# 256-channel deformable slots: early corners behind the last weighted sums, late corners in the first three taps, the first block's side rows over two taps

## The chip, the cores and the metric

One core of one Trainium2 chip. The metric is the device time of the whole kernel in microseconds. The core has five engines that run side by side and meet at semaphores: TensorE (PE), VectorE (DVE), ScalarE (ACT), GpSimd (POOL) and the DMA queue of SP.

## What is computed

Four layers follow each other on an input of 2 x 256 x 64 x 64 in float32: attention with a group norm, a positional term, a deformable bottleneck of 64 channels, and, as layer 3, two deformable convolutions of 256 channels. The change touches only layer 3, which is, for each of the two images:

```
h = relu(group_norm(x, gn1))
h = deform_conv(h, dw1, pw1, pwb1, w1, b1)
h = relu(group_norm(h, gn2))
h = deform_conv(h, dw2, pw2, pwb2, w2, b2)
return h + x
```

A deform_conv first makes two offsets for each of 9 taps at each pixel (a 7x7 depthwise convolution times a 1x1 one). Tap k is then read at a shifted, fractional place: the four pixels around it, each weighted by its share. The output is the product of the 9 x 256 sampled values with w (256 x 256 x 9).

## The kernel before

**Turns.** Layer 3 runs as four turns of `products256` (TensorE), `copies256` (ScalarE), `sums256` (VectorE) and `gathers256` (GpSimd): turn 0 is image 1 with the first deform_conv, turn 1 image 0 with the first, turn 2 image 1 with the second, turn 3 image 0 with the second. Between two turns all engines meet: each drains and signals, and SP lets them go (`meet`, L377 for SP). After the barrier VectorE works out the group norm of the image just made (`group_norm`, L1643), with one product by TensorE (L767) and one root by GpSimd (`inverse_root`, L582) inside; turn 3 needs none. SP starts the loads of a turn after its barrier: 4 MB of residual before turns 2 and 3, 2.3 MB of weights before turns 0 and 2.

**A tap.** A turn has 8 blocks of 512 pixels, a block 9 taps (k = 0 to 8), 72 taps in all. For a tap GpSimd issues four indirect gathers (`gathered`, L690, issue L696), each of which fetches for 128 pixels the four corners of 256 channels (0.5 MB). There are twelve gather tiles `G3`, three taps' worth, so the gathers of tap j + 3 are issued when tap j has been used (`half_done`) and ScalarE has copied their indices into `IS3` (L1475, semaphore `is_ready`). ScalarE multiplies the first corner by its weight (L1466), VectorE adds the other three (L2052: twelve instructions a tap, two halves of six), TensorE turns the result round (`transposes`, L1145), ScalarE copies that out of PSUM (`staged`, L1484), and TensorE multiplies it by the weights (`tap`, L1155, eight instructions a tap). The body of a tap on TensorE (`staged_tap`, L1163) is: wait for the copies of tap j, transposes of tap j + 1, a piece of the side work, matmuls of tap j. ScalarE is written tap by tap in order: products of tap j, copies of tap j - 1, side work. After a block's last tap ScalarE evicts the output (`output`, L1494 or L1499) and VectorE takes statistics of it (L2065) or adds the residual (L2040).

**Side work.** Turns 0 to 2 also prepare the next turn (`side`), one block at a time: ScalarE normalises the next image (L1355, L1369) and copies tiles of it (L1359, L1367), TensorE transposes those for the gather table (`side_table3`, L1032, two parts) and makes the offsets' 14 rows (`side_rows3`, L1040, two instructions each), VectorE adds the rows up shifted (`side_shifts3`, L1928 and L1934, waits for row 14), TensorE moves them to pixels (L984), VectorE adds them to the base (L1944). Block 0 of the side work is done before tap 0 of TensorE (`products256`: two table parts, all 14 rows, then the transposes of tap 0), block n + 1 beside block n.

**Corners.** VectorE turns offsets into whole indices and weights: `corner_floors` (L1731 to L1748, six instructions), `corner_indices` (L1754, L1758), `corner_weights` (L1766 to L1785, five). Each instruction waits for the one before. They come in two parts, `EARLY = 5`: blocks 0 to 4 of the next turn, and blocks 5 to 7. The early part is done in the last block of a turn, after taps 3, 4 and 6 (`early_corners`, L2074; in turn 0 also the two offset weights, L1886, after taps 2 and 3). The late part is done in the second block of the next turn, after taps 0, 2 and 5 (`late_corners`, L2087). Turn 0's own corners are done ahead of it. With the early indices there (`corners_done`), ScalarE copies in its last three taps the indices of the next turn's taps 0 to 2, and GpSimd issues their twelve gathers, from the next table (`following`), before it goes to the barrier.

Of the kernel before, what the change touches and what calls it, by code (L numbers as in the profile page):

```python
# [21 lines left out]
CH = C // 128  # L22
# [7 lines left out]
KK = 9  # L30
# [16 lines left out]
def program(nc, x, wqkv, wproj, pos_l, pos_r, vec, vec64, w1, woff, boff, w2, w3, dw, pw, wd,  # L47
            ident, mean32, mean8, sel2, sel3, base2, base3, out):
    ctx = ExitStack()
    with ctx:  # L50
# [512 lines left out]
        def _(pool):  # L563
# [136 lines left out]
            def gathers256(b, begins, following):  # L700
# [56 lines left out]
        def _(pe):  # L757
# [379 lines left out]
            def products256(side, new_weights=False):  # L1137
# [35 lines left out]
                def beside(n, k, first, ahead, last):  # L1173
# [4 lines left out]
                    if k == 2:  # L1178
# [5 lines left out]
                    if k >= 2 and not last:  # L1184
# [37 lines left out]
            products256(0, True)  # L1222
# [3 lines left out]
            products256(1)  # L1226
# [3 lines left out]
            products256(0, True)  # L1230

            meet()
            products256(None)
# [5 lines left out]
        def _(act):  # L1239
# [121 lines left out]
            def side_opening(b):  # L1361

                for n in range(2):
                    for half in range(CH):
                        at = chunk(n)
                        if n == 0:
                            af(NS3[:, half, :], INNER[b][:, half, at], ACT.Relu,  # L1367
                               scale=gsc[:, half:half + 1], bias=gbi[:, half:half + 1]).then_inc(ns_ready, 1)
                        af(INNER[b][:, half, at], INNER[b][:, half, at], ACT.Relu,  # L1369
                           scale=gsc[:, half:half + 1], bias=gbi[:, half:half + 1]).then_inc(stage_ready, 1)  # L1370
                for part in range(2):
                    side_copy3(part)
                for half in range(CH):
                    side_tile(b, 1, half)
# [76 lines left out]
            def copies256(b, turn, layer, side):  # L1451
# [5 lines left out]
                def products(i, k, wraps=False):  # L1457
# [44 lines left out]
                def beside(n, k, first, ahead, last):  # L1502
# [6 lines left out]
                    if 5 <= k <= 6 and ahead:  # L1509
                        side_tile(side, n + 2, k - 5)  # L1510

                def nine(g, first=False, second=False, ahead=True, last=False):

                    for k in range(KK):
                        if k > 0 or not first:
                            products(3 * g + k // 3, k % 3, last and side is not None and k >= KK - 3)
# [6 lines left out]

                weights(0, 0)
                if turn == 0:
                    af(IS3.rearrange("p a t -> p (a t)"), IDX3[:, 0:12], ACT.Copy).then_inc(is_ready, 3)
                    side_opening(side)
                products(0, 0)
                if turn == 1 or turn == 2:
                    act.wait_ge(gn_ready, 1)  # L1530
                    act.sem_inc(gn_ready, -1)
                    side_opening(side)
# [6 lines left out]
                staged(2)  # L1539
                output(NCH - 1)  # L1540
# [33 lines left out]
        def _(dve):  # L1574
# [459 lines left out]
            def sums256(b, layer, side, side_layer=0):  # L2034
# [39 lines left out]
                def early_corners(k):  # L2074

                    if k == 2 or k == 3:
                        if b == 1 and layer == 0:
                            offset_weights(1, k - 2)
                    if k == 3:
                        floors3(0, EARLY)  # L2080
                    if k == 4:
                        indices3(0, EARLY)
                        dve.sem_inc(corners_done, 1)
                    if k == 6:
# [165 lines left out]
```

## Time and profile before

| | us |
|---|---|
| median of three runs | 5462.92 |
| lowest and highest of them | 5460.71, 5473.15 |
| the profiled execution: its time | 5466.21 |
| its span | 5464.4 |

| engine | busy us | share of the span |
|---|---|---|
| TensorE matmuls | 5005.7 | 92% |
| VectorE | 4056.5 | 74% |
| GpSimd | 3392.1 | 62% |
| ScalarE | 2415.0 | 44% |

The profile is one execution; the times of its rows are in us from the span's start. The four turns fill the last third of the span, from about 3616 to 5464: turn 0 goes to about 4094, turn 1 to 4575, turn 2 to 5056. A timeline row gives start, length, engine, line, operation, operands, count, and in brackets how long the engine had been idle before it and what released it; instructions of one kind are merged in a row, so that neighbours may overlap by some 0.1 us. A windows row gives a stretch, its length, the busy time of TensorE matmuls, TensorE weight loads, VectorE, ScalarE and GpSimd (with the number of instructions), the granted TensorE clock (1.00 is 2.4 GHz, 0.50 is 1.2), the busy share of the DMA engines and what they moved in GB/s.

### The profile page before, as it was taken

Reading aid. Unit: us, or ns where it says so; the run is one execution under the profiler, and the core shown is the slowest. Engines: PE = TensorE matmul, PEld = TensorE weight load, DVE = VectorE, ACT = ScalarE, POOL = GpSimd, SP = SyncE. Lnnn points to the kernel's source line nnn. Section 1 sums busy time; section 2 is a strip of 40 time slices with the busy share of each in tenths; the row PEclk is TensorE's granted clock in tenths of the full one; section 3 lists DMA queues with packets and bytes.
Section 4 is the critical chain, followed back from the end, with each engine's and each line's share of the span. In section 5 each row is a group of like instructions: output and inputs, shape, how many; then the busy total and the mean of one; then the engine's idle time right before and its main releaser. Section 6 shows DMA issues by size and latency. Waiting matters only on the chain. (4 is left out here: it accounts for less than half of the span.)

```text
span 5464.4 us, 75029 instructions
## 1 busy us (share of the span) xinstructions
PE 5005.7 (92%) x23052; PEld 2329.0 (43%) x23052; DVE 4056.5 (74%) x6532; ACT 2415.0 (44%) x4301; POOL 3392.1 (62%) x2919
## 2 busy tenths in 40 slices
PE   7999999999799999999978869969998997999888
PEld 3333333333333333333336656745544554554444
DVE  4888888885488888888533334458987897998898
ACT  2455555554245554555411111125544554554555
POOL 0676777766067677777627757746654564666675
PEclk9999999999899999999968879989999999999999
DMA  2000000000100000000044435569997998999998
GB/s 74 1 1 1 1 1 1 1 1 16 48 1 1 1 1 1 1 1 1 2 107 120 128 106 157 164 221 385 370 361 297 375 375 331 382 383 378 385 410 356
DMA packets 320000, 812.09 MB, mean 149 GB/s; under 512 B 69934, under 2 KB 137396, under 8 KB 319470
## 3 DMA queue, kind: packets, MB, share of 16 engines
q0 software_dynamic: 193536, 679.59, 33.2%
q1 hardware_dynamic: 126190, 129.07, 7.0%
q8 instruction: 145, 2.38, 0.2%
q14 instruction: 129, 1.06, 0.1%
HBM read 708.09 MB, written 100.43 MB: 148 GB/s over the span
## 5 line engine op out<-in xcount | busy, mean ns | idle before, releaser
L647 POOL TENSOR_TENSOR arena<-arena 128x512 f32<-128x512 f32 x960 | 1438.4, 1498 | 576.6 <-ACT arena L1281 495.8
L696 POOL DMA_INDIRECT arena<-corners,arena x1152 | 1101.0, 956 | 695.4 <-DVE arena L2052 332.7
L1813 DVE TENSOR_REDUCE arena<-ps 128x2 f32<-128x1024 f32 x1024 | 1252.2, 1223 | 354.7 <-PE ps L806 351.7
L1281 ACT ACTIVATE arena<-ps 128x1024 f32<-128x1024 f32 x1024 | 1045.9, 1024 | 1061.0 <-PE ps L832 1033.5
L2052 DVE SCALAR_TENSOR_TENSOR ps<-arena,ps 128x256 f32<-128x256 f32 x2304 | 956.5, 484 | 178.8 <-DVEq L2046 170.8
L1155 PE MATMUL ps<-arena 128*128 128x512 f32 x2304 | 1060.8, 604 | 0.2
L832 PE MATMUL ps<-arena 64*128 64x512 f32 x4096 | 1046.0, 589 | 0.0
L845 PE MATMUL ps<-arena 128*64 128x512 f32 x4096 | 991.3, 605 | 0.0
L1835 DVE TENSOR_TENSOR arena<-arena 128x512 f32<-128x512 f32 x960 | 877.9, 914 | 104.4 <-ACT arena L1281 102.9
L684 POOL DMA_INDIRECT arena<-corners,arena x576 | 547.0, 950 | 276.9 <-issue 246.2
L1466 ACT ACTIVATE ps<-arena 128x256 f32<-128x256 f32 x1152 | 499.0, 469 | 473.1 <-DVE arena L2052 190.5
L1155 PEld LDWEIGHTS ps<-arena 128*128 128x128 f32 x2304 | 437.3, 195 | 502.3 <-issue 501.4
L2052 DVE SCALAR_TENSOR_TENSOR arena<-arena,ps 128x256 f32<-128x256 f32 x1152 | 499.6, 476 | 0.0
L845 PEld LDWEIGHTS ps<-arena 128*64 128x64 f32 x4096 | 248.5, 136 | 583.0 <-issue 354.3
L832 PEld LDWEIGHTS ps<-arena 64*128 64x128 f32 x4096 | 390.4, 187 | 241.5 <-issue 159.9
L1145 PE MATMUL ps<-ident_s,arena 128*128 128x128 f32 x2304 | 332.5, 280 | 151.0 <-DVE arena L2052 141.6
L1970 DVE TENSOR_TENSOR arena<-arena,ps 128x2304 f32<-128x2304 f32 x64 | 163.5, 2554 | 401.3 <-DMA arena<-corners,arena 401.0
L1484 ACT ACTIVATE arena<-ps 128x512 f32<-128x512 f32 x576 | 308.7, 586 | 234.9 <-ACTq L1482 231.4
L1145 PEld LDWEIGHTS ps<-ident_s,arena 128*128 128x128 f32 x2304 | 265.5, 143 | 344.8 <-DVE arena L2052 211.5
L828 PE MATMUL ps<-arena 64*128 64x512 f16 x2048 | 389.1, 377 | 18.7 <-ACT arena L1281 18.7
L806 PE MATMUL ps<-arena 64*128 64x512 f16 x2048 | 394.4, 382 | 4.8 <-DVE arena L1813 2.7
L806 PEld LDWEIGHTS ps<-arena 64*128 64x128 f16 x2048 | 98.5, 93 | 587.0 <-DVE arena L1813 529.2
(169 smaller groups left out, 3865.0 us busy)
## 6 DMA issues: line engine op xcount, KB each, us to landing
corners<-arena SPq DMA_DIRECT2D x256, 256.0 KB
arena<-corners,arena POOLq DMA_INDIRECT x1728, 7.7
img<-in_x SPq DMA_DIRECT2D x8, 1024.0 KB, 9.3
corners<-arena SPq DMA_DIRECT2D x128, 64.0 KB, 2.2
arena<-in_wd SPq DMA_DIRECT2D x2, 2304.0 KB, 8.5
between<-img SPq DMA_DIRECT2D x4, 1024.0 KB, 6.3
arena<-between SPq DMA_DIRECT2D x4, 1024.0 KB, 9.1
resid<-img SPq DMA_DIRECT2D x8, 512.0 KB
```

The lines of the kernel that those rows point to most:

```text
L647: pool.tensor_tensor(SUMS[u % 2][:, 0, :], SUMS[u % 2][:, 0, :], P[n % 4][:, 0, :], ALU.add).then_inc(sum_a, 1)
L684: pool.indirect_dma_start(G2[q][:, k, :], None, table64[b], bass.IndirectOffsetOnAxis(ap=IS2[:, q, k:k + 1], axis=0)).then_inc(g2_ready[q] ...
L696: pool.indirect_dma_start(G3[4 * k + t].rearrange("p a c -> p (a c)"), None, table256[b], bass.IndirectOffsetOnAxis(ap=IS3[:, k, t:t + 1], ...
L832: last = mm(ps[:, 2 * (n % 2) + h, :], KF[u // QB][rows, kc * 128:(kc + 1) * 128], QF[u // QB][rows, (u % QB) * CHUNK:(u % QB + 1) * CHUNK ...
L845: last = mm(ps[64 * h:64 * h + 64, 6, :], V[:, kc, at:at + 64], P[n % 4][:, h, :], start=(kc == 0), stop=(kc == NT - 1), tile_position=(0, ...
L1145: last = tr(ps[:, 2 + half, t * 128:(t + 1) * 128], SAMP[k][:, t, half * 128:(half + 1) * 128], ident_s[:, :])
L1155: last = mm(ps[:, 6 + oh, :], WD[:, k, half, oh * 128:(oh + 1) * 128], ST[k % 3][:, half, :], start=(k == 0 and half == 0), stop=(k == KK ...
L1281: af(P[n % 4].rearrange("p h q -> p (h q)"), ps[:, 2 * (n % 2):2 * (n % 2) + 2, :].rearrange("p h q -> p (h q)"), ACT.Exp, scale=float(D) ...
L1466: af(ps[:, h, (t % 2) * C:(t % 2 + 1) * C], G3[4 * k + t][:, 0, :], ACT.Copy, scale=WS3[:, k, 4 * t:4 * t + 1]).then_inc(prod_ready, 1)
L1813: v.tensor_reduce(mxp[u % 2][:, :, t, j], ps[:, 4:6, :], AX.X, ALU.max).then_inc(mx_done, 1)
L1835: v.tensor_tensor(SUMS[u % 2][:, 1, :], SUMS[u % 2][:, 1, :], P[n % 4][:, 1, :], ALU.add).then_inc(sum_b, 1)
L2052: last = v.scalar_tensor_tensor(SAMP[k][:, t, :] if corner == 3 else acc, G3[4 * k + t][:, corner, :], WS3[:, k, 4 * t + corner:4 * t + co ...
```

## The change

The early corners (and in turn 0 the offset weights) go behind the last weighted sum of the turn, and ScalarE copies the twelve indices at once when they are there, so that the next turn's first twelve gathers are issued after that. The late corners go into the first block, after taps 0, 1 and 2. In the first block of turns 1 and 2 TensorE begins with the transposes of tap 0; block 0's fourteen side rows go into taps 0 and 1, seven each, the wait for the shifts from tap 2 to tap 4, and block 1's rows into taps 4 to 8, three each; VectorE's shifts go from tap 1 to tap 3 and the offsets from tap 7 to tap 8; ScalarE normalises block 1 after the table copies, and copies its tile after tap 2's products. Turn 3, which has no side work, also takes its tap 0 transposes first, as before. The core of the diff:

```diff
@@ gathers256 (GpSimd) @@
-                if following is None:
-                    pool.wait_ge(is_ready, 3)
-                    pool.sem_inc(is_ready, -3)
-                else:
+                if following is not None:
                     for k in range(3):
@@ products256, beside (TensorE) @@
+                    spread = first and turn > 0
+                    if spread and k < 2:
+                        side_rows3(side, 0, range(7 * k, 7 * (k + 1)))
-                    if k == 2:
+                    if k == (4 if spread else 2):
                         side_shifts_done()
                         if ahead:
                             side_normal_done(CH)
                     if k == (5 if first else 4):
                         side_shifted(T3[0], 7, O3, sel3_s)
-                    if k >= 2 and not last:
+                    if k >= 4 and spread:
+                        side_rows3(side, n + 1, range(3 * (k - 4), min(14, 3 * (k - 3))))
+                    if k >= 2 and not spread and not last:
                         side_rows3(side, n + 1, range(2 * (k - 2), 2 * (k - 1)))
@@ products256, opening (TensorE) @@
+                if turn > 0:
+                    transposes(0, 0)
                 if side is not None:
                     side_table3(0)
                     side_table3(1)
                     side_normal_done(2 * CH)
+                if turn == 0:
                     side_rows3(side, 0, range(14))
-                transposes(0, 0)
+                    transposes(0, 0)
@@ side_opening (ScalarE); with_tile is False in turns 1 and 2 @@
+                for half in range(CH):
+                    af(NS3[:, half, :], INNER[b][:, half, chunk(0)], ACT.Relu,
+                       scale=gsc[:, half:half + 1], bias=gbi[:, half:half + 1]).then_inc(ns_ready, 1)
+                for half in range(CH):
+                    side_normal(b, 0, half)
+                if not with_tile:
+                    for part in range(2):
+                        side_copy3(part)
+                for half in range(CH):
+                    side_normal(b, 1, half)
+                if with_tile:
+                    for part in range(2):
+                        side_copy3(part)
                     for half in range(CH):
-                        at = chunk(n)
-                        if n == 0:
...
+                        side_tile(b, 1, half)
@@ copies256 (ScalarE) @@
-                    ahead = 3 * i + k + 3
-                    if wraps:
-                        ahead = 3 * i + k + 3 - TAPS
-                        if ahead == 0:
-                            act.wait_ge(corners_done, 1)
-                            act.sem_inc(corners_done, -1)
-                    af(IS3[:, k, :], IDX3[:, bass.ds(ahead * 4, 4)], ACT.Copy).then_inc(is_ready, 1)
+                    if not ends:
+                        af(IS3[:, k, :], IDX3[:, bass.ds((3 * i + k + 3) * 4, 4)], ACT.Copy).then_inc(is_ready, 1)
...
+                    if first and turn > 0 and k == 2:
+                        for half in range(CH):
+                            side_tile(side, 1, half)
...
                 staged(2)
+                if side is not None:
+                    act.wait_ge(corners_done, 1)
+                    act.sem_inc(corners_done, -1)
+                    first_indices()
                 output(NCH - 1)
@@ sums256 (VectorE) @@
+                def early_corners():
+
+                    floors3(0, EARLY)
+                    indices3(0, EARLY)
+                    dve.sem_inc(corners_done, 1)
+                    weights3(0, EARLY)
+                    if b == 1 and layer == 0:
+                        for half in range(CH):
+                            offset_weights(1, half)
 
                 def late_corners(k):
 
                     if k == 0:
                         floors3(EARLY, NCH)
+                    if k == 1:
+                        indices3(EARLY, NCH)
                     if k == 2:
-                        indices3(EARLY, NCH)
-                    if k == 5:
                         weights3(EARLY, NCH)
 
+                begins = not (b == 1 and layer == 0)
...
-                        if second and not (b == 1 and layer == 0):
+                        if first and begins:
                             late_corners(k)
                         if side is not None:
-                            if k == 1:
+                            if k == (3 if first and begins else 1):
                                 side_shifts3(side_layer)
-                            if last:
-                                early_corners(k)
-                            if k == 7:
+                            if k == (8 if first and begins else 7):
                                 side_offsets3(g)
...
-                nine(NCH - 1, last=True)
+                if side is not None:
+                    early_corners()
```

`first_indices` is the one copy of `IDX3[:, 0:12]` into `IS3` that turn 0 has at its start already (L1526); it signals `is_ready` by 3.

## Rows read from the trace of the kernel before

**Rows 1.** Windows, one block each: length, engine busy us, granted clock, DMA share, GB/s.
```profile
4251.10:4307.80 56.70, 54.68 (x189) 28.95 (x188) 49.38 (x119) 31.21 (x81) 32.79 (x35) 0.97 0.97 374
4516.40:4575.00 58.60, 49.53 (x164) 25.08 (x163) 54.91 (x131) 27.21 (x72) 33.55 (x36) 0.94 0.93 341
5126.50:5175.60 49.10, 41.68 (x143) 21.30 (x142) 47.85 (x124) 28.21 (x76) 34.03 (x35) 0.97 1.02 401
5223.50:5270.80 47.30, 41.75 (x146) 20.31 (x144) 44.64 (x111) 27.74 (x76) 34.69 (x36) 1.00 1.03 409
```

**Rows 2.** Timeline, VectorE, last blocks of turns 0 and 1: start, us, instruction.
```profile
4053.80 1.07 DVE L1886 TENSOR_TENSOR arena<-dw_s,pw_s 128x882 f32<-128x882 f32 x1
...
4541.99 0.34 DVE L1731 TENSOR_SCALAR arena<-arena 128x360 f32<-128x360 f32 x1
...
4545.65 1.66 DVE L2052 SCALAR_TENSOR_TENSOR ps<-arena,ps 128x256 f32<-128x256 f32 x4 [0.26 <-DVEq L2046]
...
4551.55 0.33 DVE L1754 SCALAR_TENSOR_TENSOR arena<-arena 128x180 f32<-128x180 f32 x1
...
4552.86 1.66 DVE L2052 SCALAR_TENSOR_TENSOR ps<-arena,ps 128x256 f32<-128x256 f32 x4 [0.36 <-DVEq L2046]
...
4562.27 0.34 DVE L1766 TENSOR_SCALAR arena<-arena 128x360 f32<-128x360 f32 x1
...
4565.34 1.66 DVE L2052 SCALAR_TENSOR_TENSOR ps<-arena,ps 128x256 f32<-128x256 f32 x4 [0.26 <-DVEq L2046]
```

**Rows 3.** Timeline, VectorE, between turn 0 and turn 1.
```profile
4093.27 0.87 DVE L2052 SCALAR_TENSOR_TENSOR arena<-arena,ps 128x256 f32<-128x256 f32 x2
...
4106.95 0.60 DVE L1646 BATCH_NORM_AGGREGATE mv<-bnst 128x2 f32<-128x48 f32 x2 [1.87 <-DVEq L1874]
...
4112.59 1.66 DVE L2052 SCALAR_TENSOR_TENSOR ps<-arena,ps 128x256 f32<-128x256 f32 x4 [0.35 <-DVEq L2046]
```

**Rows 4.** Timeline, GpSimd, between turn 0 and turn 1.
```profile
4110.60 0.71 POOL L582 TENSOR_TENSOR grs<-grs,minus_half 128x2 f32<-128x2 f32 x1 [13.12 <-POOLq L581]
```

**Rows 5.** Timeline, start of turn 0: VectorE, ScalarE, GpSimd.
```profile
3615.88 0.35 DVE L1731 TENSOR_SCALAR arena<-arena 128x360 f32<-128x360 f32 x1
...
3619.90 0.47 DVE L1758 CAST arena<-arena 128x180 int32<-128x180 f32 x1
...
3629.92 0.20 ACT L1526 ACTIVATE arena<-arena 128x12 int32<-128x12 int32 x1
...
3631.14 1.00 POOL L696 DMA_INDIRECT arena<-corners,arena  x1 [16.34 <-POOLq L705]
...
3645.00 0.95 POOL L696 DMA_INDIRECT arena<-corners,arena  x1 [0.30 <-DVE arena L2052]
```

**Rows 6.** Timeline, GpSimd, last block of turn 0, beside corner weights.
```profile
4081.55 1.06 POOL L696 DMA_INDIRECT arena<-corners,arena  x1 [0.30 <-issue]
```

**Rows 7.** Timeline, TensorE, first block of turn 1.
```profile
4115.04 1.08 PE L1032 MATMUL ps<-ident_s,arena 128*128 128x128 f32 x4 [6.02 <-PEq L1028]
...
4118.48 13.18 PE L1040 MATMUL ps<-img,arena 128*126 128x512 f32 x28
...
4142.90 6.03 PE L1155 MATMUL ps<-arena 128*128 128x512 f32 x8
...
4190.94 1.88 PE L1040 MATMUL ps<-img,arena 128*126 128x512 f32 x4
...
4192.65 3.60 PE L1155 MATMUL ps<-arena 128*128 128x512 f32 x8
...
4196.09 1.04 PE L1145 MATMUL ps<-ident_s,arena 128*128 128x128 f32 x8
```

**Rows 8.** Timeline, ScalarE and VectorE, first block of turn 1.
```profile
4114.65 2.21 ACT L1369 ACTIVATE img<-img,gbi,gsc 128x512 f32<-128x512 f32 x3
...
4121.44 1.65 ACT L1466 ACTIVATE ps<-arena 128x256 f32<-128x256 f32 x4
...
4132.66 4.58 DVE L1934 SCALAR_TENSOR_TENSOR arena<-ps,sel_s,arena 126x488 f32<-126x488 f32 x6
```

More of the change, by code:

```diff
@@ L1135, in products64, with products256 @@
                 four(NCH - 1, ahead=False, last=True)
-            def products256(side, new_weights=False):
+            def products256(side, turn, new_weights=False):
                 def transposes(tap, k):
@@ L1221, in _ @@
             meet()
-            products256(0, True)
+            products256(0, 0, True)
             meet()
             gn_means(mean8_s)
-            products256(1)
+            products256(1, 1)
             meet()
             gn_means(mean8_s)
-            products256(0, True)
+            products256(0, 2, True)
             meet()
-            products256(None)
+            products256(None, 3)
             meet()
@@ L1359, in side_tile, with side_opening @@
                 af(NS3[:, half, :], INNER[b][:, half, chunk(n)], ACT.Copy).then_inc(ns_ready, 1)
-            def side_opening(b):
-                for n in range(2):
-                    for half in range(CH):
-                        at = chunk(n)
-                        if n == 0:
[L1367 to L1374, printed above, removed]
+            def side_opening(b, with_tile=True):
+                for half in range(CH):
[11 more added lines that the diff above has]
+                        side_copy3(part)
+                    for half in range(CH):
+                        side_tile(b, 1, half)
             def side_copy(to, width, begins, ends):
@@ L1455, in weights, with products @@
                     af(WS3[:, k, :], W4_3[:, bass.ds(j * 16, 16)], ACT.Copy).then_inc(act_step, 1)
-                def products(i, k, wraps=False):
+                def products(i, k, ends=False):
                     act.wait_ge(act_step, 1)
@@ L1515, in nine @@
                         if k > 0 or not first:
-                            products(3 * g + k // 3, k % 3, last and side is not None and k >= KK - 3)
+                            products(3 * g + k // 3, k % 3, last and k >= KK - 3)
                         if k > 0 or not first:
@@ L1522, in nine, with first_indices @@
                             beside(g, k, first, ahead, last)
+                def first_indices():
+                    af(IS3.rearrange("p a t -> p (a t)"), IDX3[:, 0:12], ACT.Copy).then_inc(is_ready, 3)
                 weights(0, 0)
                 if turn == 0:
-                    af(IS3.rearrange("p a t -> p (a t)"), IDX3[:, 0:12], ACT.Copy).then_inc(is_ready, 3)
+                    first_indices()
                     side_opening(side)
@@ L1531, in copies256 @@
                     act.sem_inc(gn_ready, -1)
-                    side_opening(side)
+                    side_opening(side, False)
                 nine(0, first=True)
@@ L1539, in copies256 @@
                 staged(2)
+                if side is not None:
+                    act.wait_ge(corners_done, 1)
+                    act.sem_inc(corners_done, -1)
+                    first_indices()
                 output(NCH - 1)
@@ L2072, in residual_back @@
                     dve.sem_inc(x_back, -64)
[L2074 to L2084, printed above, removed]
-                        weights3(0, EARLY)
+                def early_corners():
[6 more added lines that the diff above has]
+                            offset_weights(1, half)
                 def late_corners(k):
@@ L2090, in late_corners, with nine @@
                         floors3(EARLY, NCH)
+                    if k == 1:
+                        indices3(EARLY, NCH)
                     if k == 2:
-                        indices3(EARLY, NCH)
-                    if k == 5:
                         weights3(EARLY, NCH)
-                def nine(g, first=False, second=False, last=False):
+                begins = not (b == 1 and layer == 0)
+                def nine(g, first=False):
                     for k in range(KK):
@@ L2117, in sums256 @@
                     residual_back()
-                nine(1, second=True)
-                with dve.Fori(2, NCH - 1) as g:
+                with dve.Fori(1, NCH) as g:
                     nine(g)
-                nine(NCH - 1, last=True)
+                if side is not None:
+                    early_corners()
                 if layer == 1:
```

## The prediction, made before the changed kernel was run

> **What bounds it now.** I read the windows view first, over one block (nine taps) of each kind. In a middle block of turn 1 TensorE is busy 54.7 of 56.7 us and the DMA engines at 0.97; in turn 3, which prepares nothing for a next turn, VectorE is busy 44.6 of 47.3 us and the DMA engines at 1.03 [rows 1]. So a middle block gives nothing to an edit of VectorE. The edges of the turns are different, and I read them in the timelines, engine by engine. In the last block of turn 1 TensorE falls to 49.5 of 58.6 us while VectorE is busy for 54.9: there VectorE sets the pace, and the corner instructions stand between its weighted sums [rows 2]. Behind the last sum comes the stretch in which only the end of the product runs, then the barrier and the group norm [rows 3]. GpSimd has by then issued the next turn's twelve gathers and sits idle, 13.1 us before its root [rows 4]. After the barrier comes a first block in which TensorE opens late [rows 7]. I count from T, the end of turn 0's last weighted sum (4094.1), and M, VectorE's first instruction behind the barrier (4106.95): M = T + 12.8 now, and the first weighted sum of turn 1 starts at M + 5.6 [rows 3].
>
> **Corners out of the last block.** In turn 1 VectorE leaves its sums for 3.66 us (floors), 1.31 (indices; the statistics in front stay) and 3.07 (weights), together 8.0 us [rows 2]. In turn 0 the two offset-weight products of 1.07 us go too, with their semaphore steps some 1.3 each: 10.7. VectorE is the pace-setter, has no wait between these rows, and TensorE has 9 us to spare in the block [rows 1], so I take the whole: -10.7 -8.0 -8.0 = **-26.7 us**. It can't be more. It can be less if the gathers don't keep up: at turn 3's 47.3/9 = 5.25 us a tap instead of VectorE's 4.70 (two halves of 2.35, a row of 1.66 and one of 0.87 less their overlap [rows 3]), seven taps lose 3.9 us a block, which gives 15 us as the lower end.
>
> **Corners behind the last sum.** The 7.4 us of VectorE itself (10 with the offset weights) are free: it now idles there until the last eviction at T + 9.7. What they release is not. The order becomes: floors and indices, ScalarE's copy of twelve indices, twelve gathers on GpSimd, and only then GpSimd's arrival at the barrier, because gathers256 issues all twelve before it returns. All of this stands in the trace once, at turn 0's start [rows 5]: floors and indices 3615.88 to 3620.37, 4.5 us; copy 0.2 us, and first gather 1.0 us after it; first to last gather 13.9, and the last takes 0.95. With 0.35 from VectorE to ScalarE the last gather ends at T + 4.5 + 0.35 + 0.2 + 1.0 + 14.8 = T + 20.8. From the last arrival to M the trace has 1.9 us [rows 3], so M moves from T + 12.8 to T + 22.7: +9.9 us, at three transitions **+29.7 us**. Queued behind those gathers is the root of the group norm, on the same engine [rows 4], and behind it VectorE, ScalarE and TensorE, so nothing covers the wait. At the third transition SP's residual fetch moves with the barrier too. The ends are 9.1 us (a wake-up of 0.2 in place of 1.0) and 11 (as much again for the drain), so 27 to 33. ScalarE's new wait is over at T + 4.9, and behind it only the last evictions are queued, which TensorE releases after T + 7.
>
> Here a rule speaks against the change. In the trace a gather beside the corner weights takes 1.06 us in place of 0.95 [rows 6], so I add nothing for the weights that now run beside the twelve gathers. The Trainium skill, SBUF — State Buffer, section "Who interferes with whom", has VectorE and GpSimd share a port pair under an exclusive lock, the loser blocking for the whole instruction. By the trace the sum gets under 1 us from this; by the rule more, which is a rival below.
>
> **First block of turns 1 and 2.** TensorE sets its length. From M to the end of tap 8's matmuls it takes 4196.09 - 4106.95 = 89.1 us. Its work, at full clock: nine taps of 3.44; ten sets of transposes of about 0.88; 28 side rows, two in 1.71; four table parts of 0.44; 0.8 for the shifted offsets [rows 7]: 66.2. So 22.9 us are lost, 9.5 of them before the fourteen rows start at M + 11.5 and the rest in waits and a slow stretch (the matmuls of tap 1 took 6.0 us in place of 3.6). The change puts the transposes of tap 0 first, and they need its sums, which end at M + 10.4, so TensorE reaches the tables at M + 11.0, where it now does at M + 8.1 [rows 7]. From there the two tables with the copy between them take 3.4 us, as now (4115.04 to 4118.48). ScalarE, which works in order, needs 3.0 us from the end of the second table to the products of tap 1 (4121.44 [rows 8]) with a copy, two tile copies and one normalisation between; it will have a copy and three normalisations (0.74 each [rows 8]), some 3.3. So the products start at M + 17.7, VectorE has the first half 1.1 later, and tap 1 goes from about M + 18.8 to M + 23.5, 3.3 us later after M than now. The rows, in the body of tap 0 behind the transposes of tap 1, start at M + 24.0, with 2.6 us of the work done: 21.4 us lost. Add 1.1 for their slow opening (28 instructions took 13.2 us, at 0.43 each 12.0). From there TensorE is continuous to tap 2's matmuls: rows to M + 31.1, tap 0 to 34.5, transposes 35.4, rows to 41.4, tap 1, transposes, a table part and tap 2 to 49.7. VectorE's shifts wait for row 14 and take 5.4 us (0.8 and 4.6 [rows 8]), to M + 47; ScalarE's products of tap 4 follow its first table copy, so tap 4's sums last from about M + 48.3 to 53.0, and TensorE stands some 3.5 us. The second table copy holds tap 5's products in the same way: 3.5 more, 7 in all. Lost in all 29.5 against 22.9: +7 us a turn, **+14 us**. With none of the later waits it is 0, with a slow clock for one more tap +10: 0 to +20 over both turns.
>
> The late corners (about 6.9 us of VectorE) leave the second block, where TensorE hides them: nothing. In the first block of turns 1 and 2 they lie beside TensorE's rows: nothing.
>
> **Turn 3 and the rest.** There the late corners cost now: the second block takes 49.1 us against 47.3 [rows 1]. In the first block they delay when slots come free, while the DMA engines bring 4 MB of residual first (10 us at 409 GB/s) and hide most of it. Between -1.8 and +5, I take 0. Turn 0's first block keeps its order; only the table tile of block 0 comes 0.7 us earlier on ScalarE: 0.
>
> **Sum:** -26.7 + 29.7 + 14 + 0 = +17.0 us. The profiled execution has a span of 5464.4 and a time of 5466.2 us, 3.3 above the median of the three runs shown; I put the change on the median: 5462.9 + 17.0 = **5479.9 us**. From here on, faster and slower mean by over 0.2% (10.9 us), about what a measurement of this kernel tells from no change.
>
> **Rivals.**
> (a) The first blocks cost nothing: spreading the rows lets TensorE recover all it loses at the opening. For it: VectorE's taps 2 and 3 no longer wait for the shifts. Against: TensorE is the bound, and opens its rows 12 us later. -26.7 + 29.7 = +3.0: 5465.9.
> (b) Faster: the barrier does not move. Its place is GpSimd's arrival; if the twelve gathers cost it no time, M stays at T + 12.8 and -26.7 + 14 = -12.7 gives 5450.2. It decides from an added wait of 0.6 us a transition or less (-26.7 + 14 + 1.8 = -10.9). Against it stand 14.8 us for twelve gathers, and the root behind them.
> (c) The last blocks stay bound by data, as turn 3 is: they give 15 in place of 26.7, +11.7: 5491.6.
> (d) VectorE's corner weights (3.1 us [rows 2]) and in turn 0 the offset weights (2.1) keep GpSimd from issuing while they run: 3 x 3.1 + 2.1 = 11.4 us of later barriers, 5491.3. Against it is the row of 1.06 us [rows 6]. That is what the rule of the Trainium skill named above (SBUF — State Buffer) would do here.
>
> **Chances.** Forecast 0.60, (a) 0.20, (b) 0.05, (c) 0.08, (d) 0.07. About 0.05 of the forecast's own 0.60 lies under 5473.8, where both first blocks come out near their lower end. So slower 0.55 + 0.08 + 0.07 = 0.70, same 0.25, faster 0.05. The range reaches from just under (a) to just over (c) and (d), which also takes in the forecast with its first blocks at +20 and its barriers at 33 (-26.7 + 33 + 20 = 26.3, 5489): 5464 to 5495.
>
> **What would show it.** Right: no corner instruction among the last block's sums, and that block at about 50.6 us; twelve gathers between T + 6 and T + 21; the root's idle time small before the gathers and the first group-norm instruction near T + 22.7; in turns 1 and 2 TensorE's rows starting at M + 24 and tap 8 ending near M + 96. Wrong: a first group-norm instruction before T + 17, or a first block under 89 us.

## The result, and the profile after

The changed kernel takes **5501.82 us** (median of four runs, 5499.76 to 5503.2) where the kernel before took 5463.19 beside it: 1.0067 times as long (95% interval 1.005 to 1.0084), 38.6 us slower. The forecast was 5479.9 in a range of 5464 to 5495. The direction was right; the loss is 2.3 times the forecast one.

The profiled execution of the changed kernel has a span of 5501.1 us, 36.7 above the one before. No engine does more work:

```profile
span 5501.1 us, 75087 instructions
PE 5003.4 (91%) x23052; PEld 2332.9 (42%) x23052; DVE 4055.7 (74%) x6532; ACT 2412.9 (44%) x4292; POOL 3385.3 (62%) x2919
```

So all of it is waiting. The windows view, block by block as in [rows 1]: a middle block of turn 1, its last block, and the second and fourth blocks of turn 3.

```profile
4267.80:4324.50 56.70, 54.68 (x189) 28.62 (x188) 49.37 (x119) 31.17 (x81) 32.71 (x36) 0.97 0.99 384
4532.30:4581.90 49.60, 46.02 (x167) 24.09 (x165) 49.04 (x119) 26.75 (x69) 23.79 (x26) 1.00 0.85 330
5165.30:5213.50 48.20, 42.40 (x147) 20.66 (x145) 44.74 (x112) 27.65 (x75) 35.28 (x38) 1.00 1.03 410
5260.80:5308.10 47.30, 41.70 (x146) 20.30 (x144) 44.60 (x111) 27.68 (x76) 34.74 (x36) 1.00 1.03 410
```

The last block is 49.6 us in place of 58.6, with VectorE busy for 49.04 of them: it still sets the pace, without the corner work. What was gained there is lost at the barrier. The timeline of VectorE between turn 0 and turn 1, against [rows 2, 3]:

```profile
4085.63 0.86 DVE L2066 SCALAR_TENSOR_TENSOR arena<-arena,ps 128x256 f32<-128x256 f32 x2
4086.41 0.34 DVE L1745 TENSOR_SCALAR arena<-arena 128x360 f32<-128x360 f32 x1
...
4090.42 0.48 DVE L1772 CAST arena<-arena 128x180 int32<-128x180 f32 x1
...
4096.53 1.29 DVE L2079 BATCH_NORM_STATS2 bnst<-img 128x6 f32<-128x512 f32 x2
4117.26 0.60 DVE L1660 BATCH_NORM_AGGREGATE mv<-bnst 128x2 f32<-128x48 f32 x2 [19.43 <-DVEq L1888]
...
4122.90 1.66 DVE L2066 SCALAR_TENSOR_TENSOR ps<-arena,ps 128x256 f32<-128x256 f32 x4 [0.35 <-DVEq L2060]
```

The last sum ends at T = 4086.49, the floors and indices behind it take until 4090.9, the last statistics are done at 4097.8, and then VectorE stands for 19.4 us: M = 4117.26 = T + 30.8, where the forecast had T + 22.7. (At the barrier before turn 3, which has no group norm, M is ScalarE's first instruction behind it.) GpSimd in the same stretch, against [rows 4, 5]:

```profile
4092.33 1.09 POOL L696 DMA_INDIRECT arena<-corners,arena  x1 [16.91 <-POOLq L711]
...
4106.26 0.95 POOL L696 DMA_INDIRECT arena<-corners,arena  x1 [0.30 <-issue]
4120.91 0.71 POOL L582 TENSOR_TENSOR grs<-grs,minus_half 128x2 f32<-128x2 f32 x1 [13.70 <-POOLq L581]
```

The twelve gathers stand where they were forecast, T + 5.8 to T + 20.7. But M doesn't follow the last of them by 1.9 us, it follows by 10.0. In between only their data moves, as 2-us windows show (the last two columns are the DMA engines' share and GB/s); its last packet ends at 4112.6:

```profile
4110.00:4112.00 2.00, 0.00 (x0) 0.00 (x0) 0.00 (x0) 0.00 (x0) 0.00 (x0) 0.50 0.93 373
4112.00:4114.00 2.00, 0.00 (x0) 0.00 (x0) 0.00 (x0) 0.00 (x0) 0.00 (x0) 0.50 0.02 6
```

The kernel before has nearly the same distance. Its twelfth gather ends at 4097.49, and its M of 4106.95 [rows 3] is 9.5 us behind that:

```profile
4096.54 0.95 POOL L696 DMA_INDIRECT arena<-corners,arena  x1 [0.30 <-issue]
```

TensorE and ScalarE at the opening of turn 1, against [rows 7, 8]:

```profile
4128.65 1.06 PE L1029 MATMUL ps<-ident_s,arena 128*128 128x128 f32 x4
...
4141.75 7.57 PE L1037 MATMUL ps<-img,arena 128*126 128x512 f32 x14
...
4210.73 3.60 PE L1152 MATMUL ps<-arena 128*128 128x512 f32 x8
```
```profile
4134.99 1.65 ACT L1474 ACTIVATE ps<-arena 128x256 f32<-128x256 f32 x4
```

Counted from M: the first table 11.4 (forecast 11.0), tap 1's products 17.7 (17.7), the rows 24.5 (24.0), the end of tap 8's matmuls 97.1 (96).

**Where the 36.7 us come from**, by T, M and the end of each block's evictions on ScalarE in both traces:

| term | forecast | measured |
|---|---|---|
| last blocks of turns 0, 1, 2, to T | -26.7 | -10.7 -8.1 -8.0 = -26.8 |
| barriers, M - T | +29.7 | 12.8, 12.9, 12.9 to 30.8, 29.9, 30.6: +52.7 |
| first blocks of turns 1 and 2, from M | +14 | +7.7 +7.8 = +15.5 |
| all else | 0 | -4.7 |

The last line is -7.9 in the second to seventh blocks (-3.1 in the second blocks of turns 1 and 2; -3.4 in their sixth, which ran 56.6 us at a granted clock of 0.97 before and 54.9 at 1.00 after; the rest in turn 3), +0.6 in turn 0's first block and turn 3's edges, and +2.6 at the start of the layer and behind the last eviction, outside all edits. The barrier's term is 23 us off, and that is the miss.

### The profile page after: what moved, and what is told of

Same layout as the page of the kernel before. It is cut to its first block and busy times, and to the rows that moved or that the text cites. A ratio compares the mean times of both kernels' runs of the same rounds, so it can differ in the third digit from the quotient of the medians.

```text
span 5501.1 us, 75087 instructions
## 1 busy us (share of the span) xinstructions
PE 5003.4 (91%) x23052; PEld 2332.9 (42%) x23052; DVE 4055.7 (74%) x6532; ACT 2412.9 (44%) x4292; POOL 3385.3 (62%) x2919
## 5 line engine op out<-in xcount | busy, mean ns | idle before, releaser
L1152 PE MATMUL ps<-arena 128*128 128x512 f32 x2304 | 1047.5, 598 | 0.2
```

The lines of the kernel that those rows point to most:

```text
L1152: last = mm(ps[:, 6 + oh, :], WD[:, k, half, oh * 128:(oh + 1) * 128], ST[k % 3][:, half, :], start=(k == 0 and half == 0), stop=(k == KK ...
```

## The experiments

The theory after this reading: `drain` in GpSimd's `meet` doesn't end before the data of the gathers ahead of it has landed. Rivals: the drain takes a fixed time behind the last issue, or another engine arrives late. Medians are given with their ratio to the kernel before, run on the same chip; M and T are read from each run's trace.

**No drain.** At the three barriers behind the gathers GpSimd arrives with a plain increment:

```diff
-                pool.drain().then_inc(arrived, 1)
+                pool.sem_inc(arrived, 1)
```

> The changed kernel, with GpSimd signalling its arrival at the three barriers between the turns without draining first. T is the end of a turn's last weighted sum, M the first group-norm instruction behind the barrier; in the changed kernel M = T + 30.8, 29.9 and 30.6, while the last of the twelve gathers has been issued at T + 20.7 and the gathers' data ends at about T + 25.5. Theory 'landing' (GpSimd's drain holds until the data of its gathers is there) and theory 'fixed' (the drain takes some 8 us behind an indirect DMA, whatever the data): M = T + 22.6 at each, 8 us less three times, so 24 us under the changed kernel, about 5478. Theory 'other engine' (something else arrives last): M stays at T + 30, 5502.

5474.96 us, 1.0021 (1.0011 to 1.0031), 27 below the changed kernel. M - T is 12.2 and 12.5 at the first two barriers and 17.1 at the third. At the first two the barrier's whole loss is GpSimd's drain, and no other engine is late. At the third 4 us are left, and they are SP's: before it arrives, it waits until the last output store has landed (`fo_sent`, L541). SP issued that store here:

```profile
5066.16 1.12 SPq L490 DMA_DIRECT2D out_y<-img  x2
```

Its packets share the DMA engines with the gathers' and end at 5074.0, with M at 5074.8; in the kernel before they end at 5068.3, with M at 5069.2. The drain's removal isn't all gained, because the root of the group norm now stands behind the gathers. VectorE and GpSimd, turn 0 to 1:

```profile
4099.59 0.60 DVE L1663 BATCH_NORM_AGGREGATE mv<-bnst 128x2 f32<-128x48 f32 x2 [0.86 <-DVEq L1891]
...
4109.04 0.16 DVE L1691 TENSOR_TENSOR gsc<-grs,vec_s 128x2 f32<-128x2 f32 x1 [5.89 <-DVEq L1690]
```
```profile
4107.20 0.94 POOL L699 DMA_INDIRECT arena<-corners,arena  x1 [0.30 <-issue]
4108.16 0.73 POOL L582 TENSOR_TENSOR grs<-grs,minus_half 128x2 f32<-128x2 f32 x1
```

The first weighted sum is at M + 10.6 in place of M + 5.6. The wait has moved from the barrier to the root.

**A quarter of the bytes.** Drain kept; each of the twelve gathers ahead of the barrier fetches a quarter of its row, so the first three taps of turns 1 to 3 are computed from other data:

```diff
-                        G3[4 * k + t].rearrange("p a c -> p (a c)"), None, table256[b],
+                        G3[4 * k + t].rearrange("p a c -> p (a c)")[:, 0:part * C], None,
+                        table256[b].rearrange("r (q c) -> (r q) c", c=part * C),
```

> The changed kernel, its drain kept, with each of the twelve gathers ahead of a barrier fetching a quarter of the bytes (one corner's worth of each row, so the first three taps of turns 1 to 3 are computed from other data). The number of gathers and their issue times stay. Theory 'landing': the data ends some 2 us behind the last issue, M = T + 20.7 + 2 + 5.2 = T + 28, about 3 us less three times, 9 us under the changed kernel: 5493. Theory 'fixed': M stays at T + 30.5, 5502. A later start of tap 1 or 2 isn't expected under either.

5498.43 us, 1.0061 (1.0044 to 1.0078). The total falls between the two theories. By the trace M - T is 28.8, 27.9 and 27.6, so 2.0, 2.0 and 3.1 us less, while the data ends 3.5 to 4.4 us earlier, counted from T. It moves with the landing, but not by the full amount: open until the crowded runs below.

**The first block as before.** Only TensorE's, ScalarE's and VectorE's order in the first blocks is undone:

```diff
-                    spread = first and turn > 0
+                    spread = False
...
-                            if k == (3 if first and begins else 1):
+                            if k == 1:
```

> The changed kernel with the first block of turns 1 and 2 as before the change (side rows ahead of the transposes of tap 0, shifts after tap 1, ScalarE's opening in one piece); early corners behind the last sum and late corners in taps 0 to 2 stay. From M to the first eviction the changed kernel takes 95.5 and 95.9 us, the kernel before 87.8 and 88.1. If the order of the opening is what costs: 15.5 us under the changed kernel, 5486. If it is the late corners beside the first taps, or the colder TensorE behind a longer barrier: no more than 3 us less, 5499.

5484.99 us, 1.0038 (1.0023 to 1.0052): 16.8 less than the changed kernel. From M to the first eviction it is 88.0 and 88.6 us, against 95.5 and 95.9 changed and 87.8 and 88.1 before. The new order costs 7 to 8 us a turn and gives nothing back, by itself; this is the forecast's +14.

**Split.** Old first block, no drain, and only tap 0's four gathers ahead of the barrier:

```diff
                 if following is not None:
-                    for k in range(3):
+                    for k in range(1):
...
```

The gathers of taps 1 and 2 are issued behind the barrier, and behind the root where there is one.

> A version meant to keep only what gains: x3_oldfirst, with the gathers of tap 0 alone ahead of the barrier, those of taps 1 and 2 behind the group norm's root, and no drain on GpSimd at the three barriers. GpSimd arrives at about T + 11, with the last eviction, so M = T + 12.8 as before the change. Theory: the last blocks' 30 us (11.9 + 9.2 + 9.2 by the evictions) and some 7 us of the middle blocks stay, nothing is paid at the barriers: 5463 - 33 = 5430. Rival: taps 1 and 2, whose data lands only some 14 us behind M, hold the first blocks 5 us each: 5445. If the barrier is held by something that these edits don't touch: over 5460.

5455.03 us, 0.9988 (0.9979 to 0.9998), a gain of 8.5 us where 33 were expected. M - T is 11.9, 10.4 and 16.8. Turn 1's first block holds at 88.5 us, turn 2's takes 98.0 (88.1 before) and turn 3's 67.6 (57.4). ScalarE at the opening of turn 2, then SP:

```profile
4571.22 0.87 ACT L1479 ACTIVATE ps<-arena 128x256 f32<-128x256 f32 x2 [1.88 <-DMA arena<-corners,arena]
4580.48 0.87 ACT L1479 ACTIVATE ps<-arena 128x256 f32<-128x256 f32 x2 [8.38 <-issue]
```
```profile
4569.24 0.35 SPq L533 DMA_DIRECT2D arena<-in_wd  x1
4569.65 3.27 SPq L484 DMA_DIRECT2D img<-resid  x4
```

The second half of tap 0 is multiplied 8.4 us late, though its last gather was issued by 4569.6: the weights (2.36 MB) and the residual (4 MB) are issued at M. Split by queue, the packets show which of the two it is: from 4572.2 to about 4580 SP's queue moves 2.37 MB, which is the weights alone, while the gathers' queue gets some 0.07 MB a us, and tap 0's 2.1 MB are through at about 4580. The kernel before has its twelve gathers landed by then. The early issue was worth something after all, as cover against transfers that come with the barrier.

**Old first block and no drain, nothing split** (all twelve gathers stay ahead of the barrier).

> The changed kernel with the first block's old order and without GpSimd's drain, all twelve gathers still issued ahead of its arrival. Theory: the two costs are independent, so it stands 16 to 17 below the run without the drain: about 5459, with M - T at 12 and the first weighted sum at M + 10 (the root of the group norm sits behind the twelfth gather). Rival: the late root already covers the opening that the old order saves, so only a few us come back: about 5470.

5461.35 us, 0.9999 (0.9989 to 1.0009). 13.6 below the run without the drain alone: the two costs are nearly independent. M - T is 12.2, 12.5 and 16.7, and the late root leaves first blocks of 92.7 and 98.1.

**The kernel before without the drain.**

> The kernel before, with GpSimd's drain at the three barriers behind the gathers replaced by a plain arrival. Theory (the last evictions and statistics set the barrier of before): no change, 5463, M - T at 12.8. Rival (the drain binds in before as well, since M stands 4.9 to 5.3 behind the end of the gathers' data there too): each barrier moves earlier, by what the data was late; at turn 2 to 3, where the data ends last, by 2 us or more, 5458 to 5461 in all.

5460.08 us, 0.9994 (0.9985 to 1.0004): no difference that can be told. In its trace M - T is 11.5, 11.5 and 12.9 in place of 12.8, 12.9 and 12.9. That is the rival at the first two barriers: VectorE's group norm now starts 0.57 us behind its last statistics, where [rows 3] has 1.87.

```profile
4105.41 0.60 DVE L1649 BATCH_NORM_AGGREGATE mv<-bnst 128x2 f32<-128x48 f32 x2 [0.57 <-DVEq L1877]
```

So the M of T + 12.8 in the kernel before looked like a barrier set by the last statistics, but GpSimd's drain came 1.3 to 1.4 us behind them. At the third barrier SP's wait for the last output store comes last, with the drain or without.

**The split with little residual.** Of each quarter of the residual only a sixteenth is fetched:

```diff
-                    at = slice(i * PIX // 4, (i + 1) * PIX // 4)
+                    at = slice(i * PIX // 4, i * PIX // 4 + PIX // 64)
```

> The split version (old first block, no drain, only tap 0 gathered ahead of the barrier) with the residual's fetch cut to a sixteenth of its 4 MB at the turns 2 and 3, so the output of the residual sum is left out for most pixels. Theory (in the split version the gathers of taps 1 and 2 share the DMA engines with the residual behind the barrier, which makes the first blocks of turns 2 and 3 98 and 68 us long where before has 88 and 57): they fall to about 88 and 58, 5436 in all. Rival (the late issue itself holds them, not the residual): 5452 to 5455.

5447.7 us, 0.9968 (0.9956 to 0.9981). Turn 3's first block falls from 67.6 to 60.0 us, so there it was the residual. Turn 2's falls only from 98.0 to 96.2, and its half of tap 0 still waits 8.4 us; what is left in front of it is the weights' fetch, which only turn 2 has and whose packets fill the same 8 us here. A run with a smaller fetch of the weights was not made. The total, 5447.7, lies between the two expectations.

**A crowd, one block too early.** SP writes the weights (2.36 MB) to an unused DRAM buffer, meant for T + 6, to delay the gathers' data and not their issue:

```diff
+                sp.wait_ge(evicted, CH * NCH)
+                sp.dma_start(hog, WD.rearrange("p k h c -> p (k h c)")).then_inc(hogged, 16)
```

> The changed kernel, with a transfer of 2.36 MB more (the convolution's weights written to an unused DRAM buffer) issued by SP when the last evictions are done, about T + 6, at the transitions 0 to 1 and 1 to 2. It delays the gathers' data by its 5.8 us at 409 GB/s and leaves GpSimd's issues where they are. Theory (GpSimd's drain holds until the gathers' data has landed): M - T goes from 30.8 and 29.9 to 35 to 37 in both, about 5512 in all. Rival (the drain takes a fixed time behind the last issue): M - T stays within 1 us of 30, 5502 to 5504.

> The same added transfer, without GpSimd's drain. It tells whether SP's own drain waits for the added transfer, which would spoil the run above. Theory: only GpSimd's drain counts, M - T stays at 12 to 13 at both transitions, and the total is 5475 plus at most 12 for later data of the first taps. Rival (SP's drain waits for what SP issued): M - T at 20 or more at the first two transitions.

A miss in both: `evicted` starts each turn at 2, not at 0, so the transfer left one block early and met none of the twelve gathers:

```profile
4046.31 0.35 SPq L388 DMA_DIRECT2D hog<-arena  x1
```

5506.64 us (1.0082, 1.0064 to 1.0101) with the drain and 5478.19 (1.0032, 1.0019 to 1.0044) without; M - T stays at 30.5 and 30.0, and at 12.2 and 12.5.

**The crowd at the right place** (`CH * NCH + CH`), with the drain:

> The added transfer of 2.36 MB again, now really behind the last evictions (in the first trial it left one block earlier, at 4046.3, so the gathers met no crowd and M - T stayed at 30.5 and 30.0). Theory (GpSimd's drain holds until the gathers' data has landed): the data ends about 5.8 us later, T + 31, and M follows it by 5, T + 36, at both transitions; about 5513 in all. Rival (a fixed time of 9 to 10 us behind the last issue): M - T stays at 30 to 31 while the data ends later, 5502 to 5506.

5513.9 us (5508.94 and 5518.86; 1.0082, 1.0052 to 1.0112). SP, GpSimd, VectorE and the windows, turn 0 to 1, with T = 4080.90:

```profile
4089.45 0.35 SPq L388 DMA_DIRECT2D hog<-arena  x1
```
```profile
4100.68 0.94 POOL L712 DMA_INDIRECT arena<-corners,arena  x1 [0.30 <-issue]
4119.71 0.71 POOL L598 TENSOR_TENSOR grs<-grs,minus_half 128x2 f32<-128x2 f32 x1 [18.09 <-POOLq L597]
```
```profile
4116.06 0.60 DVE L1676 BATCH_NORM_AGGREGATE mv<-bnst 128x2 f32<-128x48 f32 x2 [23.83 <-DVEq L1904]
```
```profile
4108.00:4110.00 2.00, 0.00 (x0) 0.00 (x0) 0.00 (x0) 0.00 (x0) 0.00 (x0) 0.50 1.02 408
4110.00:4112.00 2.00, 0.00 (x0) 0.00 (x0) 0.00 (x0) 0.00 (x0) 0.00 (x0) 0.50 0.37 147
```

The last gather is issued at T + 20.7, as in the changed kernel. The last packet of its queue ends at T + 30.4 in place of T + 26.1 (the added transfer's own ended at 4098.8), and M is at T + 35.2 (34.7 at the second barrier). From the last issue's end to M it is 14.4 us where it was 10.0; from the last packet it is 4.7 in both. The drain waits for the landing. The same crowd without GpSimd's drain:

> The same without GpSimd's drain: whether SP's own drain waits for the transfer that SP added. Theory: it doesn't, M - T stays at 12 to 13 at both transitions. Rival: M - T of 18 or more, and then the run above says nothing of GpSimd's drain.

5479.55 us (1.0029, 1.0017 to 1.004), M - T of 12.2 and 12.5. SP's own drain didn't wait for the transfer it had issued: its packets end at 4101.2, and M is at 4095.5. So the delay above is GpSimd's. All the readings together, in us; the data's end is that of the last packet in the gathers' own queue before M, and the spread kernel is the one after the table:

| run, barrier | last gather's end | data end | M | M - data end |
|---|---|---|---|---|
| before, 0 to 1 | 4097.49 | 4102.30 | 4106.95 | 4.65 |
| before, 1 to 2 | 4578.34 | 4583.72 | 4587.89 | 4.17 |
| changed, 0 to 1 | 4107.21 | 4112.60 | 4117.26 | 4.66 |
| changed, 1 to 2 | 4602.65 | 4607.64 | 4611.81 | 4.17 |
| changed, 2 to 3 | 5096.95 | 5102.95 | 5107.14 | 4.19 |
| crowded, 0 to 1 | 4101.62 | 4111.34 | 4116.06 | 4.72 |
| crowded, 1 to 2 | 4602.99 | 4612.78 | 4617.00 | 4.22 |
| spread, 0 to 1 | 4093.97 | 4100.40 | 4105.07 | 4.67 |
| spread, 1 to 2 | 4568.03 | 4574.41 | 4578.57 | 4.16 |
| spread, 2 to 3 | 5044.53 | 5051.37 | 5055.58 | 4.21 |
| quarter, 0 to 1 | 4107.81 | 4109.22 | 4115.81 | 6.59 |
| quarter, 1 to 2 | 4603.22 | 4604.59 | 4610.24 | 5.65 |
| quarter, 2 to 3 | 5097.62 | 5099.10 | 5104.61 | 5.51 |

With full rows M stands 4.2 to 4.7 us behind the last packet, and at each barrier the kernels agree within 0.1 us, the kernel before among them; from the last gather's end it varies from 9.2 to 14.4. Of this tail the barrier itself takes some 0.6 (the 0.57 above). The quarter's 5.5 to 6.6 say that with little data something else in it lasts 7 to 8 us from the last gather's end; what that is stays open. Why the first barrier's tail is 0.5 us longer stays open too.

**Early corners spread over two earlier blocks.** The kernel before, with the early corners neither in the last block nor behind it:

```diff
-                    if k == 3:
+                    if block == NCH - 3 and k == 3:
                         floors3(0, EARLY)
-                    if k == 4:
+                    if block == NCH - 2 and k == 3:
                         indices3(0, EARLY)
                         dve.sem_inc(corners_done, 1)
-                    if k == 6:
+                    if block == NCH - 2 and k == 6:
                         weights3(0, EARLY)
```

> The kernel before, with the early corners neither in the last block nor behind the last sum, but the floors in the sixth block, indices and weights in the seventh (both paced by TensorE, VectorE busy for 49.6 of 55.0 us); the two offset-weight products of turn 0 stay in the last block. Theory: the last blocks fall to about 44 (47 in turn 0), the sixth and seventh stay at 55, the barrier and the first blocks stay: 5463.5 - 9.3 - 9.2 - 9.2 = 5436. Rival: VectorE has no real room in those blocks (53.2 and 54.0 of 55 busy, in strict order with TensorE), each is 2 to 4 us longer, 6 blocks: about 5450 to 5455.

5450.83 us, 0.9976 (0.9967 to 0.9986): a gain of 12.8 us, half of the 27 expected. Windows of the sixth, seventh and last block of turn 0:

```profile
3937.70:3994.90 57.20, 54.80 (x189) 28.86 (x188) 51.77 (x125) 30.39 (x79) 34.50 (x37) 0.97 0.99 383
3994.90:4049.40 54.50, 52.81 (x189) 28.06 (x188) 52.24 (x126) 29.04 (x77) 33.84 (x36) 1.00 0.95 368
4049.40:4096.00 46.60, 40.27 (x145) 21.04 (x144) 39.96 (x94) 23.01 (x60) 27.46 (x30) 1.00 0.96 362
```

The seventh takes 54.5 as before, the sixth 57.2 where before has 54.9 to 56.6, the last falls by 9.3 (8.0 and 8.2 in turns 1 and 2). But M - T grew from 12.8 to 15.1, 14.2 and 15.3. VectorE, turn 0 to 1:

```profile
4098.52 1.29 DVE L2065 BATCH_NORM_STATS2 bnst<-img 128x6 f32<-128x512 f32 x2 [8.50 <-ACT img L1494]
4105.07 0.60 DVE L1646 BATCH_NORM_AGGREGATE mv<-bnst 128x2 f32<-128x48 f32 x2 [5.26 <-DVEq L1874]
```

VectorE waits 5.26 us behind its last statistics where it waited 1.87: the last block ends earlier, the gathers' data less so, and the drain holds the barrier for longer. So the spread corners and the plain arrival together:

> The version with the early corners in the sixth and seventh block, without GpSimd's drain at the three barriers. There M - T was 15.1, 14.2 and 15.3 with the drain, where before has 12.8. Theory (with a last block of 45 us the gathers' data ends after the last eviction, and the drain now sets the barrier): M - T falls to 11.5 to 12.5, 8 us in all, 5443. Rival (something else makes it 15): no change, 5451.

5445.96 us, 0.9968 (0.9958 to 0.9979). M - T is 10.4, 10.4 and 12.7, VectorE waits 0.57 us at the first two barriers, and the first blocks hold at 87.3 and 87.7:

```profile
4098.97 0.60 DVE L1649 BATCH_NORM_AGGREGATE mv<-bnst 128x2 f32<-128x48 f32 x2 [0.57 <-DVEq L1877]
```

This beats both kernels, by 17 us over the one before and by 56 over the changed one. Last, the one harmless part of the change on top of it, the late corners in the first block:

> The version above with one part of the change added, the late corners in the first three taps of the first block in place of the second block. My account of the change had this at nothing for turns 1 and 2 and -1.8 to +5 for turn 3. Theory (nothing, since TensorE paces the second block and the data the third turn's first): within 2 us of the version above. Rival (the second blocks of the turns 1 and 2 fall from 56.4 to 55.0 and that of turn 3 by 1, while the first blocks hold): 4 us less than the version above, about 5439.

5445.02 us, 0.997 (0.9959 to 0.998). The second blocks of turns 1, 2 and 3 do fall, from 57.0, 56.5 and 48.7 to 55.0, 55.1 and 48.1, 4.0 us in the two traces, with first blocks of 87.9, 87.6 and 58.1 (87.3, 87.7 and 57.9). Of the medians' difference of 0.9 us nothing can be told. The blocks speak for the rival, the total for neither. The other traces bear the blocks out: in the four kernels with the late corners in the second block, it takes 56.4 to 57.0 us in turns 1 and 2, eight times of eight; in the twelve with them in the first, 55.0 in twenty of twenty-four and 56.7 in four.

## Why the prediction was right or wrong

- **Last blocks** (-26.7): right, -26.8 by T. The row-by-row sum of what VectorE left its sums for was the whole gain, and rival (c) didn't come.
- **The gathers behind the last sum**: right to 0.1 us (T + 20.8 forecast, T + 20.7 measured).
- **From the last gather to M** (1.9 us): wrong, and it is the step that failed. "From the last arrival to M the trace has 1.9 us [rows 3], so M moves from T + 12.8 to T + 22.7", with 11 us a barrier as the upper end, "as much again for the drain". The 1.9 was taken from [rows 3] as the way from VectorE's arrival to M, but VectorE was not the last there: without GpSimd's drain the same way is 0.57 us. GpSimd's arrival isn't the end of its last instruction: it is a drain, which holds for the gathers' data and then some 4 us. Measured from the last gather's end: 10.0, 9.2 and 10.2 us, so +17.6 a barrier in place of +9.9. The trace of the kernel before had the number: 9.5 us from its twelfth gather's end to M, 4.7 from its data's end. Put on T + 20.8 it gives T + 30.3, where the measured M - T are 30.8, 29.9 and 30.6. The forecast never asked when the data lands.
- **First blocks** (+14): right, +15.5 in the traces; 16.8 came back when the old order was put back with the drain in place, 13.6 without it. Rival (a) falls: the spread rows recover nothing.
- **Turn 3 and the late corners** (0): the second blocks were not quite free. The removal was taken as hidden by TensorE; the traces of the changed kernel and of the last two runs show 1.4 to 2.0 us a turn in turns 1 and 2.
- **Rival (b)**, the barrier that doesn't move: it fell for the changed kernel, yet without the drain M does stay at T + 12 at the first two barriers, because a plain increment isn't held by queued gathers. Its mechanism needed the removal of one instruction.
- **The signs for wrong**: neither came. Both looked for a smaller loss (M before T + 17, a first block under 89 us); none was set for a barrier later than T + 23, which is where it went.
- **Rival (d)**, the locked port: the twelve gathers beside VectorE's corner and offset weights take 13.93 us from first to last start (4092.33 to 4106.26), 13.9 without that company [rows 5]. The lock that the Trainium skill describes (SBUF — State Buffer, "Who interferes with whom") doesn't show here: two of these twelve took 1.09 and 1.00 us in place of 0.94, 0.2 us in all, and the first of [rows 5] took 1.00 without that company. The same section of the Trainium skill has a TENSOR_TENSOR of VectorE not stall a transfer issued by GpSimd. Four of the five weight instructions and both offset weights are of that kind, which the forecast left out.

The Trainium skill, page DMA: Bandwidth & Descriptors, section "Anatomy of one DMA — SWDGE (gpsimd) path", puts the fixed part of one such transfer at about 2.0 us, setup and completion together. By that figure the tail behind the data would be an estimated 2 us at most; the rows show 4.2 to 4.7 from the last packet to M, of which the barrier itself takes some 0.6.

## What to carry to other kernels

Work moved behind the last use of an engine is free only if nothing that it releases stands ahead of a barrier. When an engine that issues transfers arrives at a barrier through a drain, count its arrival from the landing of its data, not from its last issue, and ask whether the barrier needs the data at all: here each half tap of gathers signals a semaphore of its own, which ScalarE waits for (L1471), and a plain arrival was enough. Look for room in blocks that another engine paces before using the transition; and when such a step shortens a stage, look at once for the wait that lay level with the old one: here GpSimd's drain, and at the third barrier the landing of the last output store.

## What the runs showed of the hardware that was not expected

- GpSimd's drain behind indirect gathers holds until their data has landed: M is 4.2 to 4.7 us behind the last packet at ten barriers of four kernels, whether the last gather's end was 9 or 14 us ago. SP's drain didn't hold for a 2.36 MB write that SP had issued 3.6 us before M: M stood at T + 12.2 there, as without the write, whose packets ended 5.7 us behind M.
- A plain increment on GpSimd isn't held by gathers queued ahead of it: without the drain the barrier opened at 4099.6 while seven of the twelve were still to be issued, up to 4108.1. The root that came next in the queue did wait for all of them.
- A transfer issued at the barrier delays gathers issued just before it: four gathers of 512 KB, all issued by 4569.6, were complete only at about 4580, beside 2.36 MB of weights issued at 4569.2.
